# Three unread matrix products a turn in the program of TensorE, in layer 2's routing

## The reference, cut to what matters

```python
def _L2_ffn_ref(x, Wr, W1s, b1s, W2s, b2s, W1p, b1p, W2p, b2p):
    shared = gelu(x @ W1s + b1s) @ W2s + b2s          # D=128, F=512
    rw = jax.nn.softmax(x @ Wr, axis=-1)              # E=8 experts
    topw, topi = jax.lax.top_k(rw, K)                 # K=2
    topw = topw / jnp.sum(topw, axis=-1, keepdims=True)
    mask = jnp.sum(one_hot(topi, E) * topw[..., None], axis=-2)
    h = gelu(jnp.einsum('bsd,edf->bsef', x, W1p) + b1p)
    priv = jnp.einsum('bsef,efd->bsed', h, W2p) + b2p
    return shared + jnp.einsum('bsed,bse->bsd', priv, mask)
...
x = x + _L2_ffn_ref(_layernorm(x, axis=-1), ...)      # 8192 tokens in all
```

## Time and profile before

| | us |
|---|---|
| median of three executions | 1888.52 (1886.25 to 1893.46) |
| the profiled execution | 1888.38 |
| its span, from the first instruction to the last | 1886.7 |
| TensorE busy with matmuls, whole kernel | 1604.3 (85%) |
| VectorE, ScalarE, GpSimd busy | 1056.2, 985.0, 770.8 |
| routing stage of layer 2 | 1001 to 1249 of the span |

### The profile page before, as it was taken

How to read it: one execution, slowest core, us unless ns; L and a number is a source line. 1 busy time by engine, 2 the same in 40 slices (tenths; PEclk the granted TensorE clock), 3 DMA queues, 4 the chain that set the end, 5 groups by cost and what they waited for, 6 DMA issues and landing times. The chain is left out here.

```text
span 1886.7 us, 41801 instructions
## 1 busy us (share of the span) xinstructions
PE 1604.3 (85%) x13019; PEld 1335.6 (71%) x13019; DVE 1056.2 (56%) x4172; ACT 985.0 (52%) x2966; POOL 770.8 (41%) x1339
## 2 busy tenths in 40 slices
PE   7978899988869997999996677699999968885774
PEld 5756677767759996888884455489999935554663
DVE  7923333347737775999996344243333357763431
ACT  5844444446647775666662222236666635442552
POOL 6700000014427772111114657435656534554454
PEclk9989999999969998999997788789999989996887
DMA  3200000000014330000004111112222242201221
GB/s 114 81 1 1 1 1 1 1 26 2 1 52 122 100 96 1 2 3 2 2 3 142 40 34 44 35 56 72 72 69 72 68 121 68 70 26 57 79 75 33
DMA packets 115355, 87.19 MB, mean 46 GB/s; under 512 B 22173, under 2 KB 106032, under 8 KB 115140
## 3 DMA queue, kind: packets, MB, share of 16 engines
q1 hardware_dynamic: 101044, 58.09, 11.2%
q0 software_dynamic: 12800, 26.01, 4.1%
q10 hardware_dynamic: 1296, 0.41, 0.1%
HBM read 56.31 MB, written 28.67 MB: 45 GB/s over the span
## 5 line engine op out<-in xcount | busy, mean ns | idle before, releaser
L1217 POOL DMA_INDIRECT scratch_made<-FEAT x136 | 153.0, 1125 | 121.2 <-DVE FEAT L1511 117.2
L1372 ACT ACTIVATE FEAT<-BANKS,FEAT 128x128 f32<-128x128 f32 x544 | 155.1, 368 | 83.6 <-PE BANKS L1325 70.1
L1072 ACT ACTIVATE EXP<-BANKS,NEGMAX 128x128 f32<-128x128 f32 x512 | 138.9, 382 | 59.2 <-DVE NEGMAX L1084 58.3
L1209 POOL DMA_INDIRECT scratch_sent<-FEAT,POS x128 | 124.7, 974 | 83.4 <-DVE POS L1449 48.2
L441 ACT ACTIVATE gates<-BANKS,EXP 128x64 f32<-128x64 f32 x384 | 97.4, 314 | 112.8 <-PE BANKS L418 112.8
L1334 PE MATMUL BANKS<-AUX,FEAT 128*128 x1088 | 144.0, 275 | 2.3 <-issue 1.8
L1325 PE MATMUL BANKS<-FEAT 128*128 128x128 f32 x1088 | 145.3, 277 | 0.0
L418 PEld LDWEIGHTS BANKS<-AUX,EXP 128*128 128x128 f32 x768 | 95.4, 191 | 69.7 <-DVE AUX L465 69.6
L1334 PEld LDWEIGHTS BANKS<-AUX,FEAT 128*128 128x128 f32 x1088 | 132.5, 192 | 2.8 <-issue 2.8
L1325 PEld LDWEIGHTS BANKS<-FEAT 128*128 128x128 f32 x1088 | 133.7, 194 | 0.0
L1001 POOL COPY EXP<-AUX 128x32 f32<-128x32 f32 x256 | 42.1, 209 | 217.0 <-PE BANKS L1047 217.0
(11 more groups left out here) (381 smaller groups left out, 4128.8 us busy)
## 6 DMA issues: line engine op xcount, KB each, us to landing
EXP<-in_L_ffn_W SPq DMA_DIRECT2D x128, 128.0 KB, 2.1
FEAT<-scratch_sent SPq DMA_DIRECT2D x136, 64.5 KB
EXP<-scratch_made SPq DMA_DIRECT2D x32, 256.0 KB
FEAT<-scratch_sent SPq DMA_DIRECT2D x72, 67.5 KB
X<-in_x SPq DMA_DIRECT2D x16, 256.0 KB, 2.9
STAGE<-in_adj SPq DMA_DIRECT2D x16, 256.0 KB, 3.3
scratch_sent<-FEAT,POS POOLq DMA_INDIRECT x192
scratch_made<-FEAT POOLq DMA_INDIRECT x136
```

The source lines that it names most:

```text
L1072: last = act.activation(tile(EXS[:, par], 4 * k + n), tile(PS[j], c), ACT.Exp, bias=NEGMAX[:, par, 4 * k + n:4 * k + n + 1])
L1209: pool.indirect_dma_start(out=sent2, out_offset=bass.IndirectOffsetOnAxis(ap=POS[:, n, b:b + 1], axis=0), in_=OUTBOX[:, i % R_SEND, n, k, ...
L1217: pool.indirect_dma_start(out=made2, out_offset=bass.IndirectOffsetOnAxis(ap=XI_I[:, t % R_IN, H:ROW2], axis=0), in_=YO[:, t % R_OUT, :], ...
L1372: last = act.activation(tile(HR[:, t % R_H], c), tile(PS[2 + t % 2], c), ACT.Gelu, bias=BT[:, c, t:t + 1])
```

## The change

TensorE's program of layer 2's routing gets a function that multiplies the identity matrix with four copies of itself side by side (512 columns) into bank 7. Nothing reads the result. The function waits for no semaphore and sets none. It is put into the list of the turn in three places with lag 0, so it runs in turns 0 to 15, 48 times in all: behind `xT`, behind `logits`, and behind `rank` and the totals, ahead of `down`. Turns 16 to 20 keep their program.

```diff
+                def keep_warm(i):
+                    pe.matmul(BANKS[:, 7, :].rearrange("p (g h) -> p g h", g=G), ident[:], ident[:].unsqueeze(1).to_broadcast([P, G, H]),
+                              start=True, stop=True)
+
                 def totals(i):
                     if i == NG - 1:
                         pe.matmul(PS[7][:, 0:E2], ones[:], CAR[:, NG % 4, 0, :], start=True, stop=True).then_inc(s.ex2_tot, 1)
                 pe.wait_ge(s.w, 16)
-                in_turn(NG, [(1, xT), (4, up), (1, logits), (3, rank), (3, totals), (5, down)])
+                in_turn(NG, [(1, xT), (0, keep_warm), (4, up), (1, logits), (0, keep_warm), (3, rank), (3, totals), (0, keep_warm), (5, down)])
```

## The result

The changed kernel takes 1949.57 us (median of four executions, 1935.64 to 1951.24), the kernel before 1890.99 beside it (1886.25 to 1898.60). The ratio is 1.0295, with a 95% interval of 1.0266 to 1.0325. The change makes the kernel 3% slower, where 1873 was forecast, with a range of 1858 to 1908. The profiled execution took 1951.24 us, 62.9 more than that of before.

What follows compares the result with a forecast made beforehand. In layer 2's routing, TensorE catches up with GpSimd's unbroken sends, its signals get stuck and the clock falls. The stage would end some 16 us earlier, less 1 us for later totals: 1888.4 - 15 = 1873 us, range 1858 to 1908.

Steps and rivals of the forecast that it cites:

- Start: Turns 0 to 3 of layer 2's routing: open products delay group 3's first send by 5.5 us, to 1065.2.
- Groups 3 to 12: Batches of layer 2's routing in turns with products: nine at 12.8 us, 115 us, so group 12 starts at 1180.4.
- short holds: Brief delays of TensorE's signals in GpSimd's batches, expected to persist; positions come 1.5 us after the last send.
- Groups 12 to 15: Last four batches: 40.4 us back to back, or one 9.5 us stall more; the middle ends at 1225.6.
- Behind the last send: End of layer 2's routing: the second stage's first load follows GpSimd's last send by 7.3 us, as before.
- TensorE's turn at full clock: Layer 2's routing: three products lengthen a turn from 10.6 to 12.4 us, above GpSimd's 11.5 us a batch.
- the product's price: Each added product in layer 2's routing takes 0.86 us at full clock, at most 1.9 us at half clock.
- the race: Layer 2's routing: TensorE catches up, GpSimd sends without pause, signals stick, all wait some 10 us, the clock falls, repeat.
- Rival A: Layer 2's routing: signals are held whatever GpSimd's pauses, all long stalls stay; 20 us more, 1909 us; chance 0.27.
- Rival B: Layer 2's routing: pace stays 14.3 us, higher clock (0.92) only pays for the products; 1889 us; chance 0.22.
- Rival C: Layer 2's routing: GpSimd's floor of 11.5 us a batch, no stall at the end; 1856 us; chance 0.06.
- D: TensorE's code: 192 added instructions, less than one block, bring at most one more stall, +10 us; chance within 0.27.

Runs made afterwards that it cites:

- s1: Changed kernel with GpSimd's two small operations (dev) moved from ahead of each batch into its middle, between four sends and four: 1875.07 us, ratio 0.9995 to the kernel before.
- p2: Changed kernel with dev in mid-batch, then a GpSimd wait for the second product of `up`: 1868.27 us, ratio 0.9939 to the kernel before.
- p3: Kernel before, without products, dev left ahead of the batch, GpSimd waiting in mid-batch for the second product of `up`: 1858.92 us, ratio 0.9904.
- t3: Changed kernel with all three products of a turn ahead of `rank`, on a chip that holds signals: 1893.09 us, ratio 1.0033 to the kernel before.
- t4: Changed kernel with all three products of a turn behind `rank`, ahead of `down`, on the chip with 1890.60 before: 1949.10 us, ratio 1.0316.
- e1: Changed kernel with only the product behind `xT`, 16 instead of 48: 1879.33 us against 1881.66 for the kernel before, ratio 0.9994.
- e5: Changed kernel without the product behind `xT`, second and third places kept: 1911.68 us against 1881.19 for the kernel before, ratio 1.0172.
- z1: Changed kernel with products but none of the 128 row sends of layer 2's routing, results not the reference's: 1835.87 us, against 1800.92 without products.

## Why the prediction was wrong

The sum was 1232.9 for the first load, and it came at 1308.3, 75.4 us later. By its terms:

- Start: group 3 at 1065.2 forecast, 1070.5 measured, +5.3, of which 2.6 come from ahead of the stage.
- Groups 3 to 12: nine batches of 12.8 us forecast, 19.7 measured, 177.6 - 115.2 = +62.4. This is the step that failed: "Between them are 12.4 us (TensorE's new turn) and 12.8 us ... I take 12.8, as short holds of the signals should persist."
- Groups 12 to 15: 45.2 us forecast, 56.5 measured (to 1304.6), +11.3. Behind the last send 7.3 forecast, 3.7 measured, -3.6.

Behind the failed step stands a reading that was half right: that signals are held while GpSimd sends "without a break", so that a pause ahead of a batch leaves a short hold at most. The pauses came, 7 to 12 us ahead of nearly every batch. With them no copy of `xT` that fell into the batches 3 to 12 was late by 10 us, as happened in the kernel before beside batches sent back to back. TensorE's idle stretches above 6 us fell from four to two, as the prediction had it. But the short holds were mis-sized. `xT` ended 3.7 to 5.7 us into each of these batches, and its copy came 2.1 to 3.5 us late. TensorE stood for 3.3 to 5.3 us ahead of the next batch and worked at half clock behind it, which the forecast has in no turn from group 3 on; the two turns beside each other give 2.8 us for the longer stall and 5.2 for the clock.

A wait or a pause within the batch shortens this (s1, p2, p3), and so does taking the products from behind `rank` (t3 against t4). The product behind `xT`, by itself, cost nothing (e1); what it adds to the other two was compared only across calls (30 us without it in e5, 59 with it). The prediction counted the product ahead of `down` as 0.86 us of TensorE's turn: it never asked at which time of the batch the signals would come.

Right were: TensorE's turn at full clock (12.4 us forecast; 11.6 without sends, 12.9 with the pause), the product's price, that the products make TensorE slower than the batches and end the race, and that GpSimd would wait ahead of nearly every batch. The forecast pace of 12.8 was met where the holds are short (12.87 in s1, the 11.6 us of a turn without sends and a stall of 1.25).

Rival A had the direction, slower, but not the mechanism: it kept four lumps of some 10 us, and two were left, with a shorter stall in every turn between them. It gave 1909, 40 us short. Rival B is out for this kernel: the clock stayed 0.80. With the products ahead of `rank` it fits: 0.92, and the time of before within 6 us. On stalls in every round the Trainium skill (TensorE: Matmul & The Clock Gate, HAM oscillation — how this bites in real kernels) tells of a loop of products whose wait for a DMA throttles the engine anew in each round, and gives restructuring the loop as one remedy. The trace agrees as far as a stall of 3.3 to 5.3 us came in each turn here, with the clock at 0.80, and it was 0.92 when s1 made the stall 1.25 us, with the same 48 products. Rival C is, without a lump, the pace of the chip that holds nothing. D is out: z1 and s1 have the same instructions in TensorE's program.

What stays open is why a signal is late. Depth in the batch isn't all of it: in the kernel before one `xT` ended 5.5 us into batch 4, and its copy was 0.2 us late. The traces model the ends of matmuls, so they can't say whether the signal or the last part of TensorE's own work is held. Nor do they show what differs on the one chip without it.

## What to carry to other kernels

Ahead of adding work to an engine in a loop of several, find the instruction that starts the neighbour's long burst and ask which signals fall into the burst afterwards: the same 48 products cost 0.3% ahead of `rank` and 3.2% behind it. When the engines around a burst of indirect DMAs wait for "remote", try a wait in the middle of the burst for the signal that the others need; here that gave 1%, on one chip. Products that keep TensorE busy need not raise the clock: the stage had 0.80 without them and with them, where they made a stall in every turn, and 0.92 where they didn't (t3, s1). When a stall grows, count what the clock takes behind it too: 2.8 us of stall came to 8 us a turn.

## What the runs showed of the hardware

- While GpSimd issues indirect DMAs back to back, work that waits for TensorE starts later than TensorE's work ends in the trace: 1.5 us for an end 2.9 us into a batch (t3), 3.2 to 3.3 us at 5.4 (t4), 2.1 to 3.5 at 3.7 to 5.7 (the changed kernel), and some 10 where two batches stand end to end. Where nothing is held, it is 0.04 us, 9.5 us into a batch.
- This depends on the chip. In every call in which the kernel before took 1876 to 1891 us it was there, on at least four chips; in the one with 1810 us there was none of it, with the same program and sends of the same length. The same change costs 3% in the one call of the former kind where it was run (3.2% in another, with the products all behind `rank`) and 0.2% in the latter, so a verdict on such a loop needs more than one chip, and kernels are to be compared on the same one.
